# One adaLN block with sixteen-head attention on one core: all of x held in SBUF, its norm's sums made ahead, the first quad's parts moved inside SBUF, and other places in the last batch

## The reference

```
mod = silu(c) @ wmod                      # six vectors a batch: sa, ca, ga, sb, cb, gb
ga, gb = sign(g) * max(|g|, 0.25)         # both gates
h = layernorm(x) * (1 + ca) + sa
q, k, v = split(h @ w_qkv.T)              # 16 heads of 8 features
a = q @ k.T * 8 ** -0.5
a = a - max(a)                            # then "stablemax3":
s = 1 + a*(1 + a/2*(1 + a/3)) if a >= 0 else 1 / (1 - a*(1 - a/2*(1 - a/3)))
x = x + ga * ((s / sum(s)) @ v @ w_out.T + b_out)
h = layernorm(x) * (1 + cb) + sb
x = x + gb * mlp(h)                       # 128 -> 512 -> 512 -> 128, weights +1 or -1, relu
```

## Time and profile before

| | us |
|---|---|
| median of 3 runs | 712.5 (710.43 to 712.85) |
| the profiled execution, its own time | 711.12 |
| its span | 709.3 |

### The profile page before, as it was taken

How to read it: one execution, slowest core, us unless ns; L and a number is a source line. 1 busy time by engine, 2 the same in 40 slices (tenths; PEclk the granted TensorE clock), 3 DMA queues, 4 the chain that set the end, 5 groups by cost and what they waited for, 6 DMA issues and landing times.

```text
span 709.3 us, 9702 instructions
## 1 busy us (share of the span) xinstructions
PE 628.1 (89%) x3009; PEld 245.3 (35%) x3009; DVE 649.6 (92%) x807; ACT 587.7 (83%) x541; POOL 601.8 (85%) x414
## 2 busy tenths in 40 slices
PE   7486778777789999899989999999989999997898
PEld 5132222223222334233523343233423342334356
DVE  6989999999999999999999999999999999985843
ACT  2037788988899989998999989998999989987942
POOL 7229697898979999899989999899989998898740
PEclk9568999999999999999999999999999999998999
DMA  4524112241134114151135114331214113100100
GB/s 129 176 61 163 46 54 67 77 151 29 53 93 169 50 54 108 55 171 31 38 102 171 50 51 108 113 113 53 57 55 164 54 53 92 51 8 24 34 12 30
DMA packets 43719, 56.24 MB, mean 79 GB/s; under 512 B 11548, under 2 KB 27188, under 8 KB 43668
## 3 DMA queue, kind: packets, MB, share of 16 engines
q1 hardware_dynamic: 42606, 54.17, 25.7%
q10 hardware_dynamic: 1062, 1.45, 0.6%
HBM read 32.06 MB, written 18.89 MB: 72 GB/s over the span
## 4 chain that ended last, share of the span: by engine, by line
PE 45%; DVE 24%; ACT 15%; issue 13%; DMA 1%; ACTq 0%; POOL 0%; DVEq 0%; POOLq 0%
DVE cub L918 11%; DVE mx L927 10%; PE OP L564 10%; PE MB L486 9%; PE Z L532 7%; PE SA L547 7%; ACT sq L685 6%; ACT prob L696 5%; PE MB L476 2%; PE MB L499 2%; PE MB L583 1%; PE MB L454 1%; ACT hid L739 1%; DVE st L975 1%; ACT OT L747 1%
## 5 line engine op out<-in xcount | busy, mean ns | idle before, releaser
L1104 POOL TENSOR_TENSOR cub<-cub 128x2048 f32<-128x2048 f32 x128 | 460.5, 3603 | 48.3 <-DVE cub L918 48.0
L685 ACT ACTIVATE sq<-Z,shift 128x1024 f32<-128x1024 f32 x256 | 282.4, 1117 | 74.9 <-PE Z L532 73.0
L918 DVE SCALAR_TENSOR_TENSOR cub<-sq,Z 128x1024 f32<-128x1024 f32 x256 | 309.6, 1210 | 16.2 <-ACT sq L685 15.7
L927 DVE TENSOR_REDUCE mx<-SA 128x2 f32<-128x1024 f32 x248 | 301.7, 1216 | 11.0 <-PE SA L547 8.0
L696 ACT ACTIVATE prob<-cub 128x2048 f32<-128x2048 f32 x128 | 244.4, 1911 | 0.5 <-PE OP L564 0.5
L547 PE MATMUL SA<-KH,QL 64*128 64x512 f32 x496 | 121.5, 486 | 37.5 <-DVE mx L927 28.0
L532 PE MATMUL Z<-QH,KH 64*128 64x512 f32 x512 | 129.0, 500 | 17.3 <-DVE cub L918 17.0
L564 PE MATMUL OP<-prob,Vq 128*16 128x512 f32 x1024 | 135.2, 601 | 0.0
L532 PEld LDWEIGHTS Z<-QH,KH 64*128 64x128 f32 x512 | 48.3, 184 | 196.1 <-DVE cub L918 116.1
L486 PE MATMUL MB<-hid,W 128*128 128x512 f32 x192 | 108.0, 645 | 0.0
L547 PEld LDWEIGHTS SA<-KH,QL 64*128 64x128 f32 x496 | 47.3, 187 | 120.5 <-DVE mx L927 89.5
(11 more groups left out here) (194 smaller groups left out, 478.5 us busy)
## 6 DMA issues: line engine op xcount, KB each, us to landing
QL<-parts_q SPq DMA_DIRECT2D x64, 128.0 KB, 2.5
QH<-parts_q SPq DMA_DIRECT2D x64, 128.0 KB, 2.8
KH<-parts_k SPq DMA_DIRECT2D x62, 128.0 KB, 2.6
parts_q<-SQ SPq DMA_DIRECT2D x28, 256.0 KB, 2.5
parts_k<-SK SPq DMA_DIRECT2D x28, 256.0 KB, 2.7
QH<-mp SPq DMA_DIRECT2D x253, 2.0 KB
nd<-OT SPq DMA_DIRECT2D x124, 32.0 KB
xa<-L_attn_x SPq DMA_DIRECT2D x8, 256.0 KB, 4.0
```

The source lines that it names most:

```text
L685: nc.scalar.activation(sq[:, h, :], Z[:, h, :], ACT.Square, bias=shift[:, 0:1]).then_inc(s_sq, 1)
L918: nc.vector.scalar_tensor_tensor(cub[:, m % RING, h, :], sq[:, h, :], CUB_ADD, Z[:, h, :], ALU.add, ALU.mult).then_inc(s_cv, 1)
L927: nc.vector.tensor_reduce(to, unit_bank(m, u)[:, :, :], AX_X, ALU.max).then_inc(s_mx, 1)
L1104: nc.gpsimd.tensor_tensor(ff, ff, ff, ALU.mult).then_inc(s_fp, 1)
```

## The change

- **x** is loaded whole into one tile `xs`, in three DMAs at the start (batch 0; 1 to 3; 4 to 7). xa, xb, x1 and x1k are gone: x1 is written over x, and the residual's gated bias is added in place.
- **The norm's sums of x** are made in the opening: batches 0 to 3 with BN_STATS on VectorE, batches 4 to 7 on ScalarE with 16 ACTIVATE Copy and 16 ACTIVATE Square that give sums through the accumulator output. GpSimd makes all roots in three calls. In the batches only `xn` stays, on GpSimd.
- **The first quad's parts** go from SQ and SK straight to QL, QH and KH (`first_quad`), on the queues that wrote them to HBM before. For that the contraction rows are interleaved: a part's rows stand on every second partition, and the rows of maxima between them.
- **The gates** are made by GpSimd in eight instructions behind the weights; ScalarE copies their input out of PSUM. GpSimd takes over a clear of half of KH.
- **The tables**: k goes one place later, v from step 13 to step 11, y half a step to a step later, W2G from step 8 to step 0 of the next batch, gB's load to step 12.
- **The last batch**: x1 behind the last logits, x1's statistics between the two cubics, x1n on VectorE, y in a bank of its own; the last square of `cub` on VectorE; the last x1 product in two pieces by rows (96 and 32), with the division of the first 96 rows on GpSimd.

The core of the diff:

```diff
 MAIN = [
-    ("hT", 1, [(0, "c", 4)]), ("q", 1, [(0, "d", 4)]), ("k", 1, [(1, "c", 4)]),
+    ("hT", 1, [(0, "c", 4)]), ("q", 1, [(0, "d", 4)]), ("k", 1, [(1, "d", 4)]),
...
-    ("y", -2, [(11, "c", 1), (11, "d", 1), (12, "c", 1), (12, "d", 1)]),
-    ("v", 1, [(13, "c", 4)]), ("h2T", -1, [(13, "d", 4)]),
+    ("v", 1, [(11, "c", 4)]),
+    ("y", -2, [(11, "d", 1), (12, "c", 1), (12, "d", 1), (13, "c", 1)]), ("h2T", -1, [(13, "d", 4)]),
...
-    ("x1", -1, [(8, "a", 2), (8, "c", 2)]),
-    ("y", -2, [(8, "d", 1), (9, "c", 1), (9, "d", 1), (10, "c", 1)]),
+    ("x1", -1, [(8, "b", 2), (8, "c", 2)]),
+    ("y", -2, [(9, "b", 1), (9, "c", 1), (9, "d", 1), (10, "b", 1)]),
...
-           "w2g": 8, "st1": 6, "mv1": 7, "rs1": 9, "xn": 10}
+           "w2g": 0, "xn": 10}
...
+        def first_quad(eng, to, name, s_done):
+            src, places = (SQ, PLACES_Q) if name == "q" else (SK, PLACES_K)
+            for a in range(PARTS):
+                if a == 0:
+                    eng.wait_ge(s_hi, "qk".index(name) + 1)
+                else:
+                    eng.wait_ge(s_taken[name], 1)
+                for place in places[a]:
+                    eng.dma_start(to[2 * place:P:STEP_D, 0:2, :].bitcast(F32), src[0:P // NQ, a, :].bitcast(F32))\
+                        .then_inc(s_done, 16)
...
             elif first and b == B - 1:
-                pe.wait_ge(s_mp, NQ * B)
+                pe.wait_ge(s_mx, 2 * GROUPS)
...
         def pe_tail(pe):
-            pe.wait_ge(s_att, B)
+            pe.wait_ge(t_att, 1)
...
-                nc.tensor.matmul(to, num[:, t * P:(t + 1) * P], woG[:, :], start=True, stop=False)
-                mm = nc.tensor.matmul(to, ident[:, :], xb[:, t, :], start=False, stop=True)
+                nc.tensor.matmul(to, ident[:, :], xs[:, B - 1, t, :], start=(t % 2 == 0), stop=False, skip_group_check=True)
+                nc.tensor.matmul(to, num[0:LAST, t * P:(t + 1) * P], woG[0:LAST, :], start=False, stop=False,
+                                 skip_group_check=True)
+            pe.wait_ge(s_att, B)
+            for t in range(TB):
+                to = t_x1_banks[t // 2][:, t % 2, :]
+                mm = nc.tensor.matmul(to, num[LAST:P, t * P:(t + 1) * P], woG[LAST:P, :], start=False, stop=(t % 2 == 1),
+                                      skip_group_check=True)
...
             if b == FIRST and n == 1:
-                write_parts(nc.scalar, "k", 0, FIRST_QUAD)
                 act.wait_ge(s_kone, 1)
-                act.wait_ge(s_first["k"], 4 * 16)
-                read_parts(nc.scalar, KH, parts_k, 0, s_qk)
+                first_quad(nc.scalar, KH, "k", s_qk[0])
                 write_parts(nc.scalar, "k", 0, OTHER_QUADS)
+            if b == FIRST and n in (3, 6):
+                act.wait_ge(s_x[2], 16)
+                if n == 6:
+                    act.wait_ge(s_mean1, 1)
+                for i in range((B - ON_VECTOR) * TB):
+                    tile = xs[:, ON_VECTOR + i // TB, i % TB, :]
+                    scratch = hid[n // 6][:, i // TB, i % TB * D:(i % TB + 1) * D]
+                    if n == 3:
+                        mm = nc.scalar.activation(scratch, tile, ACT.Copy, accum_out=sum1[:, i:i + 1])
+                    else:
+                        mm = nc.scalar.activation(scratch, tile, ACT.Square, bias=mean1[:, i:i + 1],
+                                                  accum_out=sq1[:, i:i + 1])
+                mm.then_inc(s_sum1 if n == 3 else s_sq1, 1)
...
+        def last_square(dve):
+            dve.wait_ge(s_cv, 2 * GROUPS)
+            ff = cub[:, (GROUPS - 1) % RING].rearrange("p a n -> p (a n)")
+            nc.vector.tensor_tensor(ff, ff, ff, ALU.mult).then_inc(s_last_fp, 1)
...
+            if b == B - 1:
+                norm_late()
             cubic(s, 1)
             of_maxima(m, 2)
             maxima(m, 1)
-            misc()
+            if b < B - 1:
+                norm_sums()
...
+            nc.gpsimd.memset(KH[:, 2 * 2:2 * NQ, :].bitcast(F32), 1.0).then_inc(s_kone_late, 1)
...
+            pool_gates(pool)
+            norms_of_x(pool, False)
+            means_for_scalar(pool)
```

More of the change, by code:

```diff
@@ L58 @@
 FIRST = -1
[L59 removed]
+OTHER_QUADS = slice(1, NQ)
 CHUNKS = 4
@@ L1285, in sp_step @@
                     read_parts(sp, KH, parts_k, g, s_qk)
[L1286 to L1291 removed]
+                    read_parts(sp, QH, parts_q, g, s_qh)
             for name, off, pieces in MISC[b]:
```

324 lines of the change are left out of this document (182 added, 142 removed).

## The result

The changed kernel takes 708.27 us (median of 20 runs, 705.19 to 710.49), the kernel before 711.19 (20 runs beside it). The ratio of the two, run beside run, is 0.9949, 95% interval 0.9937 to 0.9961: 3.6 us faster (the medians are 2.9 us apart), where 9 to 10 were forecast. The time lies inside the stated range of 695 to 708.5, at its very end, and outside the 699 to 706 of the likeliest case. The profiled execution took 708.76 us, 2.4 less than the profiled one of before: span 706.9 against 709.3.

What follows compares the result with a forecast made beforehand. No engine had over 4.6 us to give in a middle batch; the chain passes between TensorE, VectorE and ScalarE. 711.1 - 2.4 - 3.5 + 0.8 - 4.1 = 701.9, plus 0.5: 702.4 us; likeliest 699 to 706, whole range 695 to 708.5.

Steps and rivals of the forecast that it cites:

- Six batches (0 to 5) times 0.59: Middle batches: VectorE no longer makes x's statistics in steps 6 and 7; -3.5 us (-1.8 to -5.2).
- so nothing, except one filler in batch 1 that may wait about 1 us: Batches' product table: moving the key product and its copy behind one pair of logits and one prob costs nothing else.
- the term of the last batch: Last batch: reordered x1, statistics and x1n bring the end earlier; -4.1 us (-1.0 to -6.0).
- what batch 6 had promised: Batch 6 before has no statistics to make: 14.02 us against batch 5's 14.61 between the same instructions.
- The v move: v product from step 13 to 11: new handover to y, 1.6 us in six batches, half taken; +0.8 (-1.5 to +3.6).
- Rival (e): Shared PSUM bank: v-to-y handover and displaced key copy miss their places, 2.6 us in six batches; 717.2 us, chance 0.07.
- Opening: Before the first scores: direct key and query transfers start logits 5.5 us earlier; net -2.4 us (-4.0 to +2.9).
- quad 1's late reads: Opening, SyncE's queue: reads behind the gate rows' write delay the ninth unit of maxima, losing 1.3 of 5.5 us.
- the step on ScalarE: Opening: 16 sums and 16 squares at 0.40 us each end at 34.0, only then three transfers of maxima; scores at 38.2.
- (a): Opening, ScalarE: accumulating instructions are short (0.309 us), so the gain is 4.0 for 2.4; 700.8 us, chance 0.15.
- The two deductions: Last batch: VectorE's last square delays the last hidden tile 1.0 us; the divided x1 product costs 0.9, 0.6 reaching the end.
- rival (c): Last batch: GpSimd's squares or VectorE's extra square take over the stall; -1.0 for -4.1, 705.5 us, chance 0.13.

Runs made afterwards that it cites:

- the pair with doubled fillers: Two unread products in place of one in batches 0 and 1's filler steps, in the changed kernel (720.34 us) and in the kernel before (724.34 us).

## Why the prediction was wrong

**Two steps failed.** The first is "Six batches (0 to 5) times 0.59", together with the sentence "so nothing, except one filler in batch 1 that may wait about 1 us". The second is the term of the last batch, -4.1, for which the runs show about -0.5 (below). In the first, batches 0 and 1 were treated as middle batches. Neither has the second layer or y to make, batch 0 has no x1 and no first layer either; in their place stand fillers in 24 steps, and TensorE loses its clock (in the kernel before the granted clock of batch 0 is 0.91). The runs put this in its place:
- the filler left at step 11, where v now stands: 2.1 us in two steps against before, 2.4 against the kernel without it (2.4 to 2.6 at equal clock);
- the filler behind the moved k: 0.5 us in batch 1;
- low stretches: batch 1 has one that it did not have (its step 7 is 7.61 us, 6.02 where there is none), batch 0 three as before, but later and the first of 10.2 us and not 6.8. The one in batch 1 is 1.6 us in the profiled execution; those of batch 0 can't be priced from one trace. It isn't a property of the change alone: each kernel's runs differ in it by several stretches.

Together 4.2 of the 5.3 by which these two batches missed the forecast. The rest is as large as the statistics' gain that was counted for them, 1.2. In batch 1 step 6 shows it (5.32 to 4.54) and step 7 takes it back (5.24 to 6.02 without a low stretch); in batch 0 low stretches hide it.

**Middle batches.** The statistics gave what batch 6 had promised: 78.36 to 77.74 with v in its old place, 0.62 a batch (0.59). From the seventh to the tenth first cubic batch 4 takes 14.01 us (14.0 forecast). The v move was mis-sized: 0.28 a batch and the whole handover, where I took half. The forecast of 77.2 to 78.4 us held (78.02). Rival (e) did not happen; neither handover exceeds 0.26 us in a middle batch.

**Opening.** Right in sum and close in its marks: 3.1 for 2.4 (over all traces of the two openings, 43.33 and 42.76 against 38.99 to 40.41, it is 2.4 to 4.3). The loads ahead did no harm: the last MB of x landed at 14.09 us (about 14 forecast), QL's four transfers between 15.71 and 17.70 (17.5 forecast), KH's last at 19.39. Right too that quad 1's late reads take a part, though it was mis-sized: from the first logits to the transposed maxima it is 13.7 us in the changed kernel and 11.4 before, so 2.2 of the gain are lost there and not 1.3. Wrong was the step on ScalarE: "only then" does it issue its transfers. At 0.29 and 0.385 us the instructions were nearer to (a), and the last square, done at 35.66, did not bound the first scores in the changed kernel. It would have, had the reads been early.

**Last batch.** The order of events was right and the size was not. Transposed maxima stand at 641.44 (641.2 forecast), transposes of x1n at 647.84 where the earlier trace rows has 653.30 (646.2 forecast). VectorE in those steps, and the third product of the first layer:

```profile
639.13 0.87 DVE L1012 BATCH_NORM_STATS2 st<-xs 128x6 f32<-128x128 f32 x4 [0.52 <-ACT xs L757]
641.44 0.20 DVE L995 STREAM_TRANSPOSE mp<-mx 128x32 f32<-128x32 f32 x1
643.07 3.15 DVE L1028 TENSOR_SCALAR x1n<-xs,mv,rs 128x128 f32<-128x128 f32 x4
661.04 1.13 PE L505 MATMUL MB<-h2T,W 128*128 128x512 f32 x2 [0.54 <-DVE QL L950]
```

Counted from the batch's first cubic, the third product of the first layer is 4.8 us earlier (72.26 to 67.47), not 5.7, and a part of that is two low stretches that only the execution of before had. At equal low time the gain up to the last cubic is 2.7 us (the pair with doubled fillers); which step takes the other 3.0 of the 5.7 stays open. x1n takes VectorE 3.15 us. The two deductions were too small: 1.3 for the square (1.0) and 0.75 for the divided product (0.6), together the 2.2 that the end is longer than before (40.8, 38.6). The square on VectorE bought nothing. This is near rival (c), which said that VectorE's extra square takes the stall over and gave the term -1.0.

So the forecast of 702.4 us had its opening and middle batches right, left two batches out, and took the gain of the last one far too large. At equal clock the miss is larger by some 2 us than the measured time shows; that the clock came out higher was luck, since nothing in the prediction counts on it. What stays open is what decides when a low stretch comes; no kernel here removed them without paying for it.

## What to carry to other kernels

Price a change in every kind of batch that the kernel has, and when a product moves in a table, move the filler table with it: a filler beside the moved v cost 1 us a step, one behind the moved k 0.5. Where the granted clock varies from run to run, compare kernels at equal mean clock beside their medians, and check whether a filler is worth what it costs by leaving it out. A piece given to another engine (here a square) or cut in two (here a product) helps only if the profile shows that the path waits for it; they cost 1.3 and 0.75 us here.
